# The adjacency tiles of the plain sums come through GpSimd's queue, rounded in the transfer, into four buffers

## The reference

```python
def _L0_gnn_ref(x, adj_a, adj_b, W_sa, a_sa, W_gcnb, b_gcnb, Wa, ba, Wb, bb):
    type_sum_a = adj_a @ x
    type_sum_b = adj_b @ x
    attn_a = sigmoid(concatenate([type_sum_a, x], axis=1) @ Wa.T + ba)
    attn_b = sigmoid(concatenate([type_sum_b, x], axis=1) @ Wb.T + bb)
    h = x @ W_sa
    scores = (h @ a_sa[0, :Hd])[:, None] + (h @ a_sa[0, Hd:])[None, :]
    e = where(adj_a != 0, exp(-leaky_relu(scores, 0.01)), 0.0)
    attn = e / (sum(e, axis=1, keepdims=True) + 1e-05)
    x_a = attn @ h
    x_b = adj_b @ (x @ W_gcnb) + b_gcnb
    return sigmoid(attn_a * x_a + attn_b * x_b)
x = layernorm(x + _L0_gnn_ref(x, adj, adj, ...), axis=-1)
```

## Time and profile before

| | us |
|---|---|
| median of 3 runs | 962.42 (961.98 to 964.37) |
| the profiled execution's own time | 962.28 |
| its span | 960.4 |
| TensorE busy | 943.9 (98%) |
| VectorE busy | 672.0 (70%) |
| ScalarE busy | 440.7 (46%) |
| GpSimd busy | 114.3 (12%) |

### The profile page before, as it was taken

How to read it: one execution, slowest core, us unless ns; L and a number is a source line. 1 busy time by engine, 2 the same in 40 slices (tenths; PEclk the granted TensorE clock), 3 DMA queues, 4 the chain that set the end, 5 groups by cost and what they waited for, 6 DMA issues and landing times. The chain is left out here.

```text
span 960.4 us, 13001 instructions
## 1 busy us (share of the span) xinstructions
PE 943.9 (98%) x4368; PEld 783.6 (82%) x4368; DVE 672.0 (70%) x1264; ACT 440.7 (46%) x798; POOL 114.3 (12%) x328
## 2 busy tenths in 40 slices
PE   9999999999999999999999999999999999999996
PEld 6888887788788888888888888888888888888875
DVE  5979878875767676676676676685675675565667
ACT  5656644442544443543453453443543443454432
POOL 0000000220120120120120120120120120111112
PEclk9999999999999999999999999999999999999999
DMA  8677532333333433433434433333433333333320
GB/s 264 185 201 227 170 105 77 109 98 99 112 105 94 124 91 107 120 96 102 121 95 105 119 100 99 110 105 93 121 105 94 109 111 87 88 105 88 94 72 33
DMA packets 139555, 109.00 MB, mean 113 GB/s; under 512 B 10337, under 2 KB 113633, under 8 KB 139489
## 3 DMA queue, kind: packets, MB, share of 16 engines
q1 hardware_dynamic: 138624, 106.74, 39.2%
q10 hardware_dynamic: 864, 1.44, 0.7%
HBM read 101.32 MB, written 6.83 MB: 113 GB/s over the span
## 5 line engine op out<-in xcount | busy, mean ns | idle before, releaser
L595 PE MATMUL bank<-e_hi,x_hi 128*128 128x512 f32 (+1 forms) x728 | 273.3, 375 | 1.4 <-DVE e_lo L774 1.1
L597 PE MATMUL bank<-e_lo,x_hi 128*128 128x512 f32 (+1 forms) x728 | 272.4, 374 | 0.0
L596 PE MATMUL bank<-e_hi,x_lo 128*128 128x512 f32 (+1 forms) x728 | 272.2, 374 | 0.0
L399 ACT ACTIVATE e_hi<-u,c_col 128x512 fp32r<-128x512 f32 (+1 forms) x182 | 126.0, 692 | 258.0 <-DVE u L762 115.2
L620 PE MATMUL bank<-x_hi,adj_r 128*128 128x512 f32 x572 | 225.0, 393 | 0.0
L621 PE MATMUL bank<-x_lo,adj_r 128*128 128x512 f32 x572 | 223.0, 390 | 0.0
L774 DVE SCALAR_TENSOR_TENSOR e_lo<-u,c_col,e_hi 128x512 fp32r<-128x512 f32 (+1 forms) x182 | 130.0, 714 | 46.5 <-ACT e_hi L399 37.5
L595 PEld LDWEIGHTS bank<-e_hi,x_hi 128*128 128x128 f32 x728 | 137.0, 188 | 27.6 <-DVE e_lo L774 2.1
L406 ACT CAST adj_r<-raw 128x512 fp32r<-128x512 f32 (+1 forms) x180 | 105.1, 586 | 115.3 <-PE bank L621 98.8
L596 PEld LDWEIGHTS bank<-e_hi,x_lo 128*128 128x128 f32 x728 | 137.0, 188 | 24.9
L597 PEld LDWEIGHTS bank<-e_lo,x_hi 128*128 128x128 f32 x728 | 137.0, 188 | 24.6
(11 more groups left out here) (119 smaller groups left out, 848.3 us busy)
## 6 DMA issues: line engine op xcount, KB each, us to landing
raw<-adj_t_dram SPq DMA_DIRECT2D x158, 256.0 KB, 2.9
adj<-adj_t_dram SPq DMA_DIRECT2D x156, 256.0 KB, 2.9
out_dram<-y SPq DMA_DIRECT2D x24, 256.0 KB, 3.3
z1s<-x_dram SPq DMA_DIRECT2D x14, 256.0 KB, 5.2
adj<-adj_t_dram SPq DMA_DIRECT2D x26, 128.0 KB, 2.2
raw<-adj_t_dram SPq DMA_DIRECT2D x22, 128.0 KB, 2.4
z2s<-x_dram SPq DMA_DIRECT2D x6, 256.0 KB, 4.6
y<-x_dram SPq DMA_DIRECT2D x6, 256.0 KB, 3.8
```

The lines of the kernel that those rows point to most:

```text
L399: nc.scalar.activation(e_hi[g % E_RING][:, 0:cols(b)], u[g % U_RING][:, 0:cols(b)], ACT.Copy, scale=c_col[:, j:j + 1]).then_inc(e_hi_ready, 1)
L595: nc.tensor.matmul(z1[k][:, 0:n], x_hi[:, j, kk], e_hi[s][:, 0:n], start=(j == 0), stop=False)
L596: nc.tensor.matmul(z1[k][:, 0:n], x_lo[:, j, kk], e_hi[s][:, 0:n], start=False, stop=False)
L597: ins = nc.tensor.matmul(z1[k][:, 0:n], x_hi[:, j, kk], e_lo[s][:, 0:n], start=False, stop=(j == TILES - 1))
```

## The change

The `raw` buffers, their semaphores, `load_raw` on SyncE and `adjacency` on ScalarE go. GpSimd gets `load_adj_r`, which loads m straight into one of four `adj_r` buffers. Since its destination is fp32r and its source f32, the transfer itself rounds. It waits until TensorE has used m - 4. GpSimd asks for the first 30 tiles in order without other work between, then follows `places()`, four chunks ahead of TensorE; `moments(t - 1)` stands at place 5 of quarter t, behind that place's load. TensorE waits for the transfer's semaphore instead of ScalarE's. All of it that matters:

```diff
-RAW_RING = 2
-ADJ_R_RING = 2
+ADJ_R_RING = 4
@@ SyncE: load_raw(m) and all its calls are taken out
-            def load_raw(m):
-                if m > LAST_CHUNK:
-                    return
-                since(sp, adj_r_ready, m - RAW_RING + 1)
...
-                sp.dma_start(raw[m % RAW_RING][:, 0:parts(m), :], source).then_inc(raw_loaded[m % RAW_RING], 16)
@@ GpSimd
-            for t in range(LAST - 1):
-                moments(t)
+            def load_adj_r(m):
+                if m > LAST_CHUNK:
+                    return
+                since(pool, adj_r_used, m - ADJ_R_RING + 1)
+                if m < TILES:
+                    source = adj_t[0:WIDE, :, m, :].rearrange("t p i -> p t i")
+                else:
+                    t, c = chunk_of(m)
+                    j, n = chunk(c)
+                    source = adj_t[t, :, j:j + n, :]
+                nc.gpsimd.dma_start(adj_r[m % ADJ_R_RING][:, 0:parts(m), :], source) \
+                    .then_inc(adj_r_loaded[m % ADJ_R_RING], 16)
+
+            for m in range(TILES + ADJ_R_RING):
+                load_adj_r(m)
+            for b, q, t, i, j, chunks in places():
+                for c in chunks:
+                    load_adj_r(chunk_number(t + 2, c) + ADJ_R_RING)
+                if i == 5 and t >= 1:
+                    moments(t - 1)
+            moments(LAST - 2)
@@ ScalarE: adjacency(m) and all its calls are taken out
-            def adjacency(m):
-                n = parts(m)
-                act.wait_ge(raw_loaded[m % RAW_RING], 16 * (m // RAW_RING + 1))
-                since(act, adj_r_used, m - ADJ_R_RING + 1)
-                nc.scalar.copy(adj_r[m % ADJ_R_RING][:, 0:n, :], raw[m % RAW_RING][:, 0:n, :]).then_inc(adj_r_ready, 1)
@@ TensorE: sum_first(j), and the same in sum_z2(m)
-                pe.wait_ge(adj_r_ready, j + 1)
+                pe.wait_ge(adj_r_loaded[s], 16 * (j // ADJ_R_RING + 1))
```

More of the change, by code:

```diff
@@ L116, in adj_resnorm_kernel @@
         adj = [sb(f"adj{s}", [P, WIDE, P]) for s in range(ADJ_RING)]
-        raw = [sb(f"raw{s}", [P, CHUNK, P]) for s in range(RAW_RING)]
         adj_r = [sb(f"adj_r{s}", [P, CHUNK, P], F32R) for s in range(ADJ_R_RING)]
@@ L166, in adj_resnorm_kernel @@
         adj_loaded = [sem(f"adj_loaded{s}") for s in range(ADJ_RING)]
-        raw_loaded = [sem(f"raw_loaded{s}") for s in range(RAW_RING)]
+        adj_r_loaded = [sem(f"adj_r_loaded{s}") for s in range(ADJ_R_RING)]
         l_saved, l_loaded = sem("l_saved"), sem("l_loaded")
@@ L176, in adj_resnorm_kernel @@
         e_hi_ready, e_lo_ready, esum_steps, e_used = sem("e_hi_ready"), sem("e_lo_ready"), sem("esum_steps"), sem("e_used")
-        adj_r_ready, adj_r_used = sem("adj_r_ready"), sem("adj_r_used")
+        adj_r_used = sem("adj_r_used")
         z1_copied, z2_copied = sem("z1_copied"), sem("z2_copied")
@@ L282, in _ @@
                 load_adj(j + ADJ_RING)
-                if FIRST_AFTER[j] is not None:
-                    load_raw(FIRST_AFTER[j] + 1)
                 if j == 7:
@@ L298, in _ @@
                     sp.dma_start(bias_row[:, :], b_gcnb.to_broadcast([P, D])).then_inc(bias_loaded, 16)
-            load_raw(TILES + 1)
             for b, q, t, i, j, chunks in places():
@@ L303, in _ @@
                     load_adj(b * TILES + j + ADJ_RING)
-                for c in chunks:
-                    load_raw(chunk_number(t + 2, c) + RAW_RING)
                 if i == 2 and t >= 2:
@@ L313, in _ @@
                         .then_inc(l_saved, 16)
-            for c in range(LAST_FIRST, CHUNKS):
-                load_raw(chunk_number(LAST, c) + RAW_RING)
             store(LAST - 3)
@@ L476, in _ @@
             piece_hi(1)
-            adjacency(0)
             copy_v(0, v_l)
             piece_hi(2)
-            adjacency(1)
             piece_hi(3)
             copy_v(1, v_r)
-            adjacency(2)
             piece_hi(4)
-            adjacency(3)
             act.wait_ge(l_spread, WIDE)
@@ L490, in _ @@
             piece_hi(5)
-            adjacency(4)
             for j in range(TILES):
@@ L497, in _ @@
                 pieces_hi(j)
-                if FIRST_AFTER[j] is not None:
-                    adjacency(FIRST_AFTER[j])
                 if j == TILES - 2:
@@ L516, in _ @@
                         steep(g + 1)
-                for c in chunks:
-                    adjacency(chunk_number(t + 2, c))
                 if i == 0 and t >= 1:
@@ L544, in _ @@
             gate_exps(LAST - 1)
-            for c in range(LAST_FIRST, CHUNKS):
-                adjacency(chunk_number(LAST, c))
             act.wait_ge(turn_done, LAST)
@@ L614, in sum_z2 @@
                 s = m % ADJ_R_RING
-                pe.wait_ge(adj_r_ready, m + 1)
+                pe.wait_ge(adj_r_loaded[s], 16 * (m // ADJ_R_RING + 1))
                 if c == 0:
```

6 lines of the change are left out of this document (removed).

## The result

| | kernel before | kernel after |
|---|---|---|
| median, us | 961.98 (960.40 to 964.37, 5 runs) | 958.97 (958.29 to 960.12, 5 runs) |
| profiled execution, us | 962.28 | 959.82 |
| its span, us | 960.4 | 958.0 |

The ratio is 0.996, with a 95% interval of 0.9941 to 0.9979: faster by 3.0 us at the medians. The forecast was 960.2 with 958.8 to 967 around it and "same" as the likeliest case; the kernel is faster, by little, and the interval leaves no room for none.

What follows compares the result with a forecast made beforehand. TensorE was taken as full (busy 943.9 of 960.4 us), leaving only its own waits, under 10 us. 962.28 - 2.7 (gain) + 0.5 (start) = 960.1, given as 960.2; range 958.8 to 967.

Steps and rivals of the forecast that it cites:

- The gain, 2.7 us: TensorE's waits removed: 1.74 and 0.5 us for esum, 0.5 us for zt_lo at tile 2's first place.
- Store of the l row at 222.98: End of block 1, SyncE's queue: without the raw load ahead, the store goes 2.6 us earlier than 225.58.
- both esum waits: TensorE's waits for esum, 1.74 us at 242.55 (end of block 1) and 0.5 us elsewhere; both were to go.
- tile 2: Its first place, 180.68: TensorE waits 1.50 us for zt_lo; 0.5 goes without the rounding copy, 1.0 stays.
- The start, 0.5 us: Opening loads: GpSimd's four early tiles may stand ahead of needed transfers; 0 to 3.8 us added, 0.5 taken.
- The chances: Overall outcome odds: faster 0.22, same 0.59 (959.5 to 965.3 us), slower 0.19.
- GpSimd's own time, 1.35 and 2.7 us: GpSimd's time per load: 1.35 us for a 128-row tile, 2.7 for block 0's 512 pieces; counted as zero cost.
- the late start: Rival: GpSimd needs 4 us per load or is slow on its first; tile 4 4.2 us late, 964 us; chance 0.13.
- GpSimd's pace: Rival: GpSimd's issuing bounds block 0, deciding from 4.6 us a load; 973 us at 5 us; chance 0.10.
- The new wait on norm: VectorE stands 0 to 5 us, 23 times, as moments follow the place 5 load; counted 0, covered by idle time.
- Slower transfer engines: Rival: rounding slows transfers in block 0, deciding at 2.3 times; 980 us at 4 times; chance 0.05.
- ScalarE near 335 us: Sign to look for: ScalarE's busy time after losing its 180 rounding copies, 105.3 us in all.

Runs made afterwards that it cites:

- the dose experiment: Changed kernel with one wait added: SyncE's store of the l row also waits until TensorE has used chunk 2 of its quarter; 1011.62 us, ratio 1.0474.
- the experiment that took it away: Changed kernel with the moments put ahead of the load at place 5 on GpSimd's queue; 959.19 us, ratio 0.9932.

## Why the prediction was wrong, point by point

*The gain, 2.7 us: right in its cause, too small in its size, and the first step that failed.* Store of the l row at 222.98 forecast and 222.96 measured; both esum waits gone; zt_lo less by 0.52, with 0.98 left where 1.0 was to stay. The kernel with the store alone moved and the dose experiment show that it is this store's place that makes the esum waits. But the term was added up from the lengths in the list of waits. Measured by the starts of the same matmuls in the two profiled executions, the places give 1.9 us (taken as 1.74) and 0.7 (taken as 0.5) at esum, 0.5 at tile 2, and 0.3 at each of two later places of the same kind, 856.24 and 887.32, which the list does not show and the forecast did not look for. That is 3.8 us for 2.7.

*The start, 0.5 us: the second step that failed.* It was taken between 0 and 3.8, and it is about 0. The terms were read rightly: the weights do come 0.7 us late. But the first z1 starts no later than before in three profiled executions of the kernel after, and about 0.3 us late in one of a kernel with the same first loads. Where the weights are waited for, their matmuls begin 0.2 to 0.3 us sooner; what gives the rest back is not shown.

*The clock behind a wait: missing from the sum, and by luck its size hides the two others.* Without the start the forecast sum is 959.6, and the profiled execution is 959.82. That is no agreement: it is 3.8 us of gain at these places and 0.2 us ahead of tile 2's first place, less the 1.6 us at 1.2 GHz behind the wait at 928.46. Of fourteen profiled executions, of the kernels here that keep this wait of 2.0 us, eight have the stretch behind it and six don't, the three of the kernel before among these. So the same wait costs 2.0 us in one execution and 3.6 in the next, and what decides it is not shown. The mean granted clock of an execution does not tell the two apart, since it also counts what comes behind the last matmul: two profiled executions of the kernel before have 0.999 and 0.997, and both are at the full level up to their last matmul.

*Why the kernel before is slower still on some chips: open.* Its median is 962.3 on one chip and 966.9 on another, and that of the kernel after 958.8 and 959.4. Its 110 executions on four chips have mean granted clocks of 0.991 to 0.999, the 23 of the kernel after 0.996 to 0.999. A lower clock goes with a longer time, but it is not the whole of it: among executions at 0.996 and 0.997, on the first of these chips twenty of the kernel before took 962.7 us in the mean and six of the kernel after 959.7; on the second ten took 966.0 and two 959.9. The theory that the esum waits, which differ from one profiled execution to the next (2.2, 1.2 and 1.8 us), bring the lower clock with them is only argued: with the store moved none of 11 executions fell under 0.996, but with the raw loads on GpSimd's queue, where no esum wait is left, one of 12 did (its trace has one stretch of lower clock at 19 to 23 us, behind waits at the start, and one at 934). No profiled execution of the kernel before is one of 965 us or more, so no trace shows where its other 3 to 4 us lie.

*The chances: wrong by the same steps.* With 0 for the start and 3.8 for the gain, the forecast stands at 958.5, or at 960.1 in an execution with the stretch of lower clock. What counts as the same began at 959.5, so "faster", which had 0.22, should have been the likelier case.

*GpSimd's own time, 1.35 and 2.7 us: too high by 2.5 and 3.6 times, and harmless.* The nearest row was two small arithmetic instructions; nearly all issues are 0.53 and 0.74 to 0.79, and the longest is 0.93. With it fall the rivals of the late start (from 3.2 us) and of GpSimd's pace (from 4.6). The first-call price of about 6 us that was weighed from the Trainium skill (GPSIMD Engine Reference, Instruction dispatch) does not show: four issues in 3.17 us. By the Trainium skill (SBUF — State Buffer, Who interferes with whom), writing descriptors is locked out beside VectorE's two-port modes, which tensor_scalar can enter. The trace goes that way, but only by a little. The median issue is 530 ns with VectorE busy for 70% of the span. From block 1 on, 19 issues begin together with VectorE's TENSOR_SCALAR for y (0.55 us), and these take 0.67 us; they also stand right behind the moments, but two that stand there without it take 0.59. Which mode VectorE was in no run shows. It makes 0.08 us for each of the 19, where TensorE never waits.

*The new wait on norm: right.* Forecast at 0 to 5 us in most quarters and worth 0; measured 45.4 us in 21, 5.4 at most, and worth nothing, by the experiment that took it away.

*Slower transfer engines: right to leave out.* 1.28 times, against the 2.3 from which it would count.

*ScalarE near 335 us: it was 356.2.* 105.3 us of copies left and only 84.5 us of busy time. The sum of single lengths is more than the busy time that they make up, for instructions overlap at their ends: in the earlier trace rows the copy at 178.24 lasts to 178.84 and the scaling starts at 178.75. It changed nothing in the time.

## What to carry to other kernels

When the bound engine is full, look for what a change does to the order of the queues, and test that part alone first: one moved store gave most of what a new queue, four buffers and 180 removed copies gave. Don't take the list of waits for the whole prize: compare the starts of the same instructions before and after, which also shows a gain in one place and a loss in another that hide each other in the total. Price a wait of the bound engine above its length: even one of 2.0 us cost 3.6 in eight of fourteen traces. And look for the room of the step that uses a late arrival before its lateness is counted.

## What the runs showed of the hardware

A wait of TensorE of 4.2 us was followed by some us of matmuls at the lower clock and cost 6.3 us in all; five of 9 us at most, 36.8 in sum, cost 52. One of 2.0 us was followed by a stretch at 1.2 GHz in eight of fourteen traces, for about 1.6 us more, and by none in six. GpSimd needs 0.53 us to issue 256 KB as 128 rows and 0.74 as 512 pieces, and 0.67 for the rows when it stands right behind the moments and beside VectorE's TENSOR_SCALAR. Rounding in the transfer takes the engines 1.15 times as long as the same transfer unrounded on the same queue; unrounded, that queue makes 13696 packets of what are 35904 rounded, or on SyncE's queue. A rounded tile lands in 3.1 us at the median (11.9 at most), the unrounded one of before in 2.9 (10.0).
